# Layer one's bias added by VectorE while the product leaves PSUM, and layer two's low half split over two slots

## The chip, the cores and the metric

The kernel runs on one core of a Trainium2 chip. The metric is the device time of one execution in microseconds; lower is better. TensorE multiplies, VectorE, ScalarE and GpSimd work on tiles, SyncE issues most of the loads, and 16 DMA engines carry them.

## What is computed

Two residual blocks follow each other on x, 2048 tokens of width 512. The first is a quantised graph layer with a dense 2048 x 2048 matrix `adj`. The second, which the change touches, is a mixture of 16 experts with two chosen per token:

```python
def _L0_ffn_ref(x, Wr, br, W1, b1, g1, be1, W2, b2):
    logits = x_flat @ Wr + br
    probs = jax.nn.softmax(logits, axis=-1)
    topk_w, topk_idx = jax.lax.top_k(probs, TOP_K)
    ...
    h = jnp.einsum('nc,ech->neh', x_flat, W1) + b1
    h = _layernorm(h, g1, be1)
    h = jax.nn.gelu(h, approximate=False)
    expert_out = jnp.einsum('neh,eho->neo', h, W2) + b2
    sel = jnp.take_along_axis(expert_out, topk_idx[:, :, None], axis=1)
    ...
x = x + _L0_gnn_ref(_layernorm(x, axis=-1), adj, ...)
x = x + _L0_ffn_ref(_layernorm(x, axis=-1)[None], ...)[0]
```

All of it is float32. b1 and b2 have 16 rows of 512, one per expert.

## The kernel before

The first block takes until about 230 us and isn't touched, apart from some bias preparation beside it. Towards its end the kernel chooses experts, sorts the tokens by expert into pages of 128 and writes a plan.

The expert stage works through the pages. A page is a **slot**; this input has 40. A word of the plan, one for two slots, says which expert each slot has and whether an expert starts there. The loops run over pairs of slots: the two halves of a loop body are the slots with `par` 0 and 1, and the plan's word is read into registers at the loop's turn. `If` on a bit of that word guards the work that is done once per expert.

Precision comes from split products: a float32 factor is cut into a high part (fp32r, copied by ScalarE) and a low part (the difference, made by VectorE). A layer on a page is then 12 matmuls of 128 x 128 by 512: high by high (line 1464), low activations by high weights (line 1467), high activations by low weights (line 1470). Ahead of them, line 1462 starts the sum in PSUM with the bias: `two_rows`, which is one in two rows, times `bias_row`, a ring of four experts whose two rows hold the bias's high and low part.

**TensorE**, slot s (`slot`): transposes of `h_hat` of page s (line 1486), layer two of page s-1, transposes of the gathered rows of page s+3 (line 1455), layer one of page s+2. That order is written by hand; each group waits on semaphores.

**VectorE** has this order in slot s, by hand as well: `h_hat` of page s+1 (line 1230), low part of the gelu output of page s (1235), low part of the rows of page s+3 (1208), statistics of layer one's product of page s+2 (`slot_stats`: 1212, 1214, 1215), then `split_next`, the low half of weights (1223), for the next expert. Layer one's is made if an expert starts at slot s+2, layer two's if one starts at slot s; each is two pieces of 128 x 1024. Seen from TensorE, the statistics and pieces of VectorE's slot s come beside TensorE's slot s+1, since they wait for the product of page s+2.

**GpSimd** takes the power of the variance (line 646), gathers rows (625) and adds the outputs to memory (650). **ScalarE** has the gelu (865), the high parts (870, 824), the gated output (830) and the high halves of the weights (837), the last when the raw weights have landed and with the same conditions on starting experts.

**SyncE** loads the weights of expert e into `w_raw`, two buffers per layer, in the fixed order layer two of e, layer one of e+1, layer two of e+1, layer one of e+2. Each load waits (line 524) until VectorE has made the low half of expert e-2 of that layer (`split_lo`), and stands in the queue behind the one before it. The bias row goes ahead of each (line 472).

```python
def load_bias(n, e, ring):
    sp.dma_start(bias_row[n][0:2, ring].bitcast(F32), bias_dram[n, e]).then_inc(raw_in[n], 16)
...
def slot(s, par, word):
    slot_h_hat(s + 1, 1 - par)
    slot_g_lo(s, par)
    slot_x_lo(s + 3, 1 - par)
    slot_stats(s + 2, par)
    split_next(0, expert_in(word, par + 2), starts_in(word, par + 2))
    split_next(1, expert_in(word, par), starts_in(word, par))
```

Of the kernel before, what the change touches and what calls it, by code (L numbers as in the profile page):

```python
# [22 lines left out]
ALU = mybir.AluOpType  # L23
# [6 lines left out]
P = 128  # L30
# [137 lines left out]
def gnn_moe_program(nc, x, adj_steps, gnn_w, scalars, wr, br, w1, b1, g1, be1, w2, b2, consts, xn_rows, bias_dram, out):  # L168
    with ExitStack() as ctx:
# [87 lines left out]
        end_gnn = where[0]  # L257
        bias_row = [place(f"bias_row{n}", [P, 4 * D], F32R) for n in (1, 2)]

# [176 lines left out]
        def _(sp):  # L436
# [34 lines left out]
            def load_bias(n, e, ring):  # L471
                sp.dma_start(bias_row[n][0:2, ring].bitcast(F32), bias_dram[n, e]).then_inc(raw_in[n], 16)

# [10 lines left out]
            def store_biases():  # L484

                sp.wait_ge(bias_ok, 1)
                for n in range(2):
                    for h, half in enumerate((bias_hi, bias_lo)):
                        sp.dma_start(bias_dram[n, :, h, :], half[32 * n:32 * n + E, :].bitcast(F32)).then_inc(bias_out, 16)

# [9 lines left out]
            for n in range(2, STEPS + WINDOWS):  # L500
                sp.wait_ge(adj_lo_ok, n - 1)
                load_adj(n)
                w = n - STEPS
                if w == BIAS_OUT_IN:
                    store_biases()
                if w == WEIGHTS_IN:
                    sp.wait_ge(bias_out, 64)
                    sp.wait_ge(bias_zero, 2)
# [23 lines left out]
        def _(pool):  # L532
# [7 lines left out]
            own.link(pool.memset(b_raw[:, :], 0.0))  # L540
            for base, b in ((0, b1), (32, b2)):
                pool.dma_start(b_raw[base:base + E, :], b).then_inc(bias_in, 16)
            pool.wait_ge(consts_in, 16)
# [20 lines left out]
            for t in range(1, T):  # L564
                x_scale(t)
                if t in (AHEAD - 1, AHEAD + 1):
                    pool.memset(bias_row[(t - AHEAD + 1) // 2][:, :].bitcast(F32), 0.0).then_inc(bias_zero, 1)
            pool.wait_ge(tables_in, 16)
# [326 lines left out]
        def _(dve):  # L895
# [119 lines left out]
            def split_bias():  # L1015

                dve.wait_ge(bias_in, 32)
# [191 lines left out]

            def slot_stats(s, par):  # L1210
                dve.wait_ge(mm1, s + 1)
                link(dve.bn_stats(h_stats[:, par, :], h_ps(par)))  # L1212
                dve.sem_inc(dve_turn, 1)
# [3 lines left out]
            def split_next(n, e, start):  # L1217

                with dve.If(start == 1):
# [5 lines left out]
                    ins.then_inc(split_lo[n], 1)  # L1225

            def slot_h_hat(s, par):

                dve.wait_ge(h_rstd, s + 1)
                dve.tensor_scalar(h_hat[:, par, :], h_ps(par), h_mv[:, par, 0:1], h_rs[:, par, 0:1], ALU.subtract, ALU.mult  # L1230
                                  ).then_inc(h_hat_ok, 1)
# [5 lines left out]

            def slot(s, par, word):

                slot_h_hat(s + 1, 1 - par)  # L1240
                slot_g_lo(s, par)
                slot_x_lo(s + 3, 1 - par)
                slot_stats(s + 2, par)
                split_next(0, expert_in(word, par + 2), starts_in(word, par + 2))
                split_next(1, expert_in(word, par), starts_in(word, par))

# [4 lines left out]
            rest = dve.value_load(pairs[0:1, 0:1], min_val=E // 2 - 2, max_val=SLOTS // 2 - 2)  # L1251
            slot_stats(0, 0)
            split(1, 0, 1)
            slot_h_hat(0, 0)
            slot_x_lo(2, 0)
            slot_stats(1, 1)
            split_next(0, expert_in(word, 1), starts_in(word, 1))
            slot(0, 0, word)
            slot(1, 1, word)
            with dve.Fori(1, SLOTS // 2 - 1) as j:  # L1260
                with dve.If(j < rest + 1):
                    own.enter(j - 1, 2 * 2)
                    word = load_plan(dve, j)
                    for par in range(2):
                        slot(j * 2 + par, par, word)
                    own.leave(0)
            word = load_plan(dve, rest + 1)
            slot_h_hat(rest * 2 + 3, 1)
            slot_g_lo(rest * 2 + 2, 0)
            split_next(1, expert_in(word, 0), starts_in(word, 0))  # L1270
            slot_g_lo(rest * 2 + 3, 1)
# [4 lines left out]
        def _(pe):  # L1276
# [181 lines left out]
            def layer(dst, n, s, par, e, act_hi, act_lo, lo_ok, done):  # L1458

                at = [bass.ds((e & 1) * (C * D) + c * D, D) for c in range(C)]  # L1460
                pe.wait_ge(split_hi[n], e + 1)
                pe.matmul(dst, two_rows[:, :], bias_row[n][:, bass.ds((e & 3) * D, D)], start=True, stop=False)  # L1462
                for c in range(C):
                    pe.matmul(dst, act_hi[:, par, c * P:(c + 1) * P], w_hi[:, n, at[c]], start=False, stop=False)  # L1464
                pe.wait_ge(lo_ok, s + 1)
# [109 lines left out]
```

## Time and profile before

| | us |
|---|---|
| median of 3 runs | 531.89 |
| lowest and highest | 531.49, 533.54 |
| the profiled execution | 533.34 |
| its span, first to last instruction | 531.6 |
| mean granted TensorE clock in it | 0.967 of full |

The page gives for each engine its busy time, digits of the busy share in 40 slices of the span (13.3 us each), and groups of instructions by source line with their mean duration and the idle time ahead of them. A matmul's duration holds its way through the array, so neighbours overlap; how long it takes from the engine is the distance to the next start. Some 40 slots of the expert stage lie between 242.6 and 520 us.

### The profile page before, as it was taken

To read this page: it belongs to the slowest core of one execution; us is meant where nothing else is said; L and a number is where in the kernel's file an instruction comes from. 1 tells how busy PE (TensorE), PEld (TensorE's weight loads), DVE (VectorE), ACT (ScalarE), POOL (GpSimd) and SP (SyncE) were. 2 spreads that over 40 slices of the span, in tenths; PEclk is the share of its full clock that TensorE was granted. 3 is DMA by queue.
4 is the path that set the end of the run, shared out by engine and by line. 5 is a ranking of instruction groups with operands and counts; after the bars stand their busy time and mean duration, and the time that the engine had idled before them with its cause. 6 is when DMAs were issued, how large, how long until landed. Compare 5 with 4: busy or idle time off the path is not lost. (4 is left out here: it accounts for less than half of the span.)

```text
span 531.6 us, 10326 instructions
## 1 busy us (share of the span) xinstructions
PE 481.1 (90%) x2328; PEld 391.1 (74%) x2329; DVE 349.1 (66%) x699; ACT 289.8 (55%) x484; POOL 227.2 (43%) x302
## 2 busy tenths in 40 slices
PE   1789999899999997678999999999999999999981
PEld 0568888788877776657788788888777888778851
DVE  5797765656557568858665786676877766776420
ACT  1656453454343343526667667668768766665540
POOL 5583520411351726334544444444444444344432
PEclk9989999999999999559999999999999999999996
DMA  8621232654787441156766776776887896644443
GB/s 285 243 81 40 80 99 78 239 208 166 251 275 259 152 170 49 37 160 203 236 160 153 201 199 151 218 167 149 239 279 206 249 279 161 141 79 80 80 62 40
DMA packets 33033, 87.75 MB, mean 165 GB/s; under 512 B 6032, under 2 KB 6176, under 8 KB 32880
## 3 DMA queue, kind: packets, MB, share of 16 engines
q1 hardware_dynamic: 18912, 56.53, 32.4%
q0 software_dynamic: 9488, 22.55, 21.0%
q10 hardware_dynamic: 4608, 8.39, 4.1%
q8 instruction: 10, 0.16, 0.1%
q14 instruction: 15, 0.12, 0.1%
HBM read 68.05 MB, written 19.40 MB: 165 GB/s over the span
## 5 line engine op out<-in xcount | busy, mean ns | idle before, releaser
L865 ACT ACTIVATE g_sb<-ps,be_sb,g_sb 128x128 f32<-128x128 f32 x160 | 60.1, 456 | 63.6 <-PE ps L1486 62.9
L625 POOL DMA_INDIRECT xg<-xn_rows,tok_i x41 | 44.6, 1087 | 116.4 <-ACT gate L844 100.0
L1329 PE MATMUL ps<-sup,adj_hi 128*128 128x512 f32 x192 | 78.3, 408 | 2.3 <-DVE adj_lo L962 2.3
L1223 DVE TENSOR_TENSOR w_lo<-w_raw,w_hi x58 | 67.8, 1221 | 17.0 <-issue 17.0
L1329 PE MATMUL ps<-sup,adj_lo 128*128 128x512 f32 x192 | 75.3, 392 | 0.0
L962 DVE SCALAR_TENSOR_TENSOR adj_lo<-adj_raw,small,adj_hi 128x1024 fp32r<-128x1024 f32 x32 | 40.7, 1273 | 39.6 <-ACT adj_hi L705 39.5
L650 POOL DMA_INDIRECT out<-y_sb,scat_i x37 | 58.9, 1592 | 16.6 <-issue 10.4
L837 ACT ACTIVATE w_hi<-w_raw x29 | 54.8, 1914 | 1.8 <-DMA w_raw<-in_w 1.0
L581 POOL TENSOR_SCALAR rstd<-mv 128x1 f32<-128x1 f32 x15 | 14.6, 974 | 91.1 <-DVE mv L1008 91.1
L1230 DVE TENSOR_SCALAR h_hat<-ps,h_mv,h_rs 128x512 f32<-128x512 f32 x40 | 32.3, 807 | 28.6 <-issue 17.5
L705 ACT ACTIVATE adj_hi<-adj_raw,small 128x1024 fp32r<-128x1024 f32 x32 | 36.8, 1149 | 22.3 <-PE ps L1329 13.5
L1212 DVE BATCH_NORM_STATS2 h_stats<-ps 128x6 f32<-128x512 f32 x40 | 27.8, 696 | 28.9 <-PE ps L1470 22.2
L1329 PEld LDWEIGHTS ps<-sup,adj_hi 128*128 128x128 f32 x192 | 36.1, 188 | 11.5 <-DVE adj_lo L962 4.9
L1464 PE MATMUL ps<-w_hi,xt_hi 128*128 (+1 forms) x160 | 44.5, 400 | 0.0
L1467 PE MATMUL ps<-w_hi,xt_lo 128*128 (+1 forms) x160 | 44.3, 399 | 0.0
L1464 PE MATMUL ps<-w_hi,gt_hi 128*128 x160 | 43.5, 393 | 0.0
L1470 PE MATMUL ps<-w_lo,xt_hi 128*128 (+1 forms) x160 | 43.2, 392 | 0.0
L830 ACT ACTIVATE y_sb<-ps,gate 128x512 f32<-128x512 f32 x40 | 27.5, 688 | 28.6 <-PE ps L1470 28.6
L1470 PE MATMUL ps<-w_lo,gt_hi 128*128 x160 | 42.9, 390 | 0.0
L1467 PE MATMUL ps<-w_hi,gt_lo 128*128 x160 | 42.8, 389 | 0.0
L1329 PEld LDWEIGHTS ps<-sup,adj_lo 128*128 128x128 f32 x192 | 36.2, 188 | 6.7
L1462 PE MATMUL ps<-bias_row,two_rows 128*128 (+1 forms) x80 | 38.7, 483 | 0.1
(181 smaller groups left out, 970.4 us busy)
## 6 DMA issues: line engine op xcount, KB each, us to landing
w_raw<-in_w SPq DMA_DIRECT2D x64, 512.0 KB
adj_raw<-in_adj_steps SPq DMA_DIRECT2D x32, 512.0 KB, 3.5
out<-x_sb ACTq DMA_DIRECT2D x16, 256.0 KB, 2.9
xn_rows<-xn ACTq DMA_DIRECT2D x16, 256.0 KB, 2.8
x_sb<-in_x SPq DMA_DIRECT2D x3, 1024.0 KB, 13.5
gw_raw<-in_gnn_w SPq DMA_DIRECT2D x1, 1024.0 KB, 5.0
x_sb<-in_x SPq DMA_DIRECT2D x2, 512.0 KB, 7.6
xg<-xn_rows,tok_i POOLq DMA_INDIRECT x41, 5.5
```

The costliest lines, as they stand in the source:

```text
L625: return pool.indirect_dma_start(to[:, s % 2, :], None, xn_rows, bass.IndirectOffsetOnAxis(ap=tok_i[:, s:s + 1], axis=0)).then_inc(landed[ ...
L650: pool.indirect_dma_start(out, bass.IndirectOffsetOnAxis(ap=at, axis=0), y_sb[:, par, :], None, compute_op=ALU.add).then_inc(scattered[par ...
L705: act.activation(adj_hi[:, par, :], adj_raw[:, par, :], ACT.Copy, scale=small[:, 0:1]).then_inc(adj_hi_ok, 1)
L837: act.activation(w_hi[:, n, at], w_raw[:, n, :, :].rearrange("p a n -> p (a n)")[:, at], ACT.Copy).then_inc(split_hi[n], 1)
L865: ins = act.activation(g_sb[:, par, c * P:(c + 1) * P], ht_ps(par)[:, c * P:(c + 1) * P], ACT.Gelu, scale=g1_sb[:, bass.ds(e_s * C + c, 1) ...
L962: dve.scalar_tensor_tensor(adj_lo[:, par, :], adj_raw[:, par, :], small[:, 0:1], adj_hi[:, par, :].bitcast(F32), ALU.mult, ALU.subtract).t ...
L1223: ins = dve.tensor_tensor(w_lo[:, n, at], w_raw[:, n, :, :].rearrange("p a n -> p (a n)")[:, at], w_hi[:, n, at].bitcast(F32), ALU.subtract)
L1329: ins = pe.matmul(acc_bank(t), part[:, n % 2, k * P:(k + 1) * P], sup[:, first_k + k, :], start=first_k + k == 0 and part is adj_hi, stop= ...
L1462: pe.matmul(dst, two_rows[:, :], bias_row[n][:, bass.ds((e & 3) * D, D)], start=True, stop=False)
L1464: pe.matmul(dst, act_hi[:, par, c * P:(c + 1) * P], w_hi[:, n, at[c]], start=False, stop=False)
L1467: pe.matmul(dst, act_lo[:, par, c * P:(c + 1) * P], w_hi[:, n, at[c]], start=False, stop=False)
L1470: ins = pe.matmul(dst, act_hi[:, par, c * P:(c + 1) * P], w_lo[:, n, at[c]], start=False, stop=c == C - 1)
```

## The change

Layer one's bias no longer passes through TensorE. `b1`'s row of an expert is loaded in fp32 to all 128 partitions (`b1_rows`, a ring of four), and VectorE adds it as it takes the product out of PSUM into a new tile `h_sb`; the statistics and `h_hat` read `h_sb`. Layer two keeps its bias matmul. The preparation of high and low bias rows is left for b2 alone.

Layer two's low half, two pieces in one slot before, becomes one piece in that slot (`begin_split`, if an expert starts at slot s) and one in the next (`end_split`, if one started at slot s-1), which also signals `split_lo`. VectorE needs two words of the plan for it.

```diff
             def load_bias(n, e, ring):
-                sp.dma_start(bias_row[n][0:2, ring].bitcast(F32), bias_dram[n, e]).then_inc(raw_in[n], 16)
+                if n:
+                    sp.dma_start(bias_row[0:2, ring].bitcast(F32), bias_dram[e]).then_inc(raw_in[n], 16)
+                else:
+                    row = e if not isinstance(e, int) else slice(e, e + 1)
+                    sp.dma_start(b1_rows[:, ring], b1[row, :].broadcast_to([P, D])).then_inc(raw_in[n], 16)
...
-            for base, b in ((0, b1), (32, b2)):
-                pool.dma_start(b_raw[base:base + E, :], b).then_inc(bias_in, 16)
+            pool.dma_start(b_raw[0:E, :], b2).then_inc(bias_in, 16)
...
-                if t in (AHEAD - 1, AHEAD + 1):
-                    pool.memset(bias_row[(t - AHEAD + 1) // 2][:, :].bitcast(F32), 0.0).then_inc(bias_zero, 1)
+                if t == AHEAD + 1:
+                    pool.memset(bias_row[:, :].bitcast(F32), 0.0).then_inc(bias_zero, 1)
...
-            def slot_stats(s, par):
+            def slot_stats(s, par, e):
                 dve.wait_ge(mm1, s + 1)
-                link(dve.bn_stats(h_stats[:, par, :], h_ps(par)))
+                link(dve.tensor_tensor(h_sb[:, par, :], h_ps(par), b1_rows[:, bass.ds((e & 3) * D, D)], ALU.add))
+                link(dve.bn_stats(h_stats[:, par, :], h_sb[:, par, :]))
...
+            def low_piece(n, e, h):
+
+                at = bass.ds(((e + 1) & 1) * (C * D) + h * (C * D // 2), C * D // 2)
+                return dve.tensor_tensor(w_lo[:, n, at], w_raw[:, n, :, :].rearrange("p a n -> p (a n)")[:, at],
+                                         w_hi[:, n, at].bitcast(F32), ALU.subtract)
+
+            def begin_split(e, start):
+
+                with dve.If(start == 1):
+                    dve.wait_ge(split_hi[1], e + 2)
+                    low_piece(1, e, 0)
+
+            def end_split(e, start):
+
+                with dve.If(start == 1):
+                    low_piece(1, e, 1).then_inc(split_lo[1], 1)
...
-                dve.tensor_scalar(h_hat[:, par, :], h_ps(par), h_mv[:, par, 0:1], h_rs[:, par, 0:1], ALU.subtract, ALU.mult
+                dve.tensor_scalar(h_hat[:, par, :], h_sb[:, par, :], h_mv[:, par, 0:1], h_rs[:, par, 0:1], ALU.subtract, ALU.mult
...
-            def slot(s, par, word):
+            def slot(s, par, word, earlier):
...
-                slot_stats(s + 2, par)
+                slot_stats(s + 2, par, expert_in(word, par + 2))
                 split_next(0, expert_in(word, par + 2), starts_in(word, par + 2))
-                split_next(1, expert_in(word, par), starts_in(word, par))
+                if earlier is not None:
+                    end_split(expert_in(earlier, 1 - par), starts_in(earlier, 1 - par))
+                begin_split(expert_in(word, par), starts_in(word, par))
...
-                    word = load_plan(dve, j)
+                    earlier, word = load_plan(dve, j - 1), load_plan(dve, j)
...
-                pe.matmul(dst, two_rows[:, :], bias_row[n][:, bass.ds((e & 3) * D, D)], start=True, stop=False)
+                if n:
+                    pe.matmul(dst, two_rows[:, :], bias_row[:, bass.ds((e & 3) * D, D)], start=True, stop=False)
                 for c in range(C):
-                    pe.matmul(dst, act_hi[:, par, c * P:(c + 1) * P], w_hi[:, n, at[c]], start=False, stop=False)
+                    pe.matmul(dst, act_hi[:, par, c * P:(c + 1) * P], w_hi[:, n, at[c]], start=not n and c == 0, stop=False)
```

Three places in the instruction order. VectorE, first half of the loop body before, from the subtraction that makes `xt_lo` to the first piece of layer one's low half:

```order
L1208 TENSOR_TENSOR xt_lo<-ps,xt_hi 128x512 [waits x_hi_ok]
L1211 REGISTER_ALU
L1212 BN_STATS h_stats<-ps 128x6 [waits mm1]
L158 ISA
L1214 BN_AGGR h_mv<-h_stats 128x2 [waits dve_own]
L158 REGISTER_ALU
L1215 TENSOR_SCALAR h_rs<-h_mv 128x1 [waits dve_own]
L1219 REGISTER_ALU x2
L1219 COMPARE_AND_BRANCH
```

The same place in the changed kernel:

```order
L1212 TENSOR_TENSOR xt_lo<-ps,xt_hi 128x512 [waits x_hi_ok]
L1215 REGISTER_ALU
L1216 REGISTER_ALU [waits mm1]
L1216 REGISTER_ALU x2
L1216 ISA
L1216 TENSOR_TENSOR h_sb<-ps,b_rows 128x512
L158 ISA
L1217 BN_STATS h_stats<-h_sb 128x6 [waits dve_own]
L158 REGISTER_ALU
L1219 BN_AGGR h_mv<-h_stats 128x2 [waits dve_own]
L158 REGISTER_ALU
L1220 TENSOR_SCALAR h_rs<-h_mv 128x1 [waits dve_own]
```

An addition and its address now stand between the wait for the product (`mm1`) and the statistics, and the wait sits on a register operation.

Second, VectorE behind layer one's pieces in the same half of the loop body. `split2_hi` is the signal of ScalarE's high half of layer two. In the changed kernel:

```order
L1224 UNCONDITIONAL_BRANCH
L1246 REGISTER_ALU x2
L1246 COMPARE_AND_BRANCH
L1235 REGISTER_ALU x4
L1235 ISA
L1235 TENSOR_TENSOR w_lo<-w_raw,w_hi 128x1024
L1246 UNCONDITIONAL_BRANCH
L1240 REGISTER_ALU x2
L1240 COMPARE_AND_BRANCH
L1241 REGISTER_ALU x2
L1235 REGISTER_ALU [waits split2_hi]
```

Where one branch led to two pieces of layer two, there are two branches with a piece each, the earlier expert's second piece first, and both behind layer one's pieces.

Third, TensorE at the head of layer one in a loop body, before:

```order
L1461 REGISTER_ALU [waits x_hi_ok]
L1461 REGISTER_ALU x2
L1462 REGISTER_ALU [waits split1_hi]
L1462 ISA
L1462 MATMUL ps<-bias_row_111,two_rows 128x512
L1464 REGISTER_ALU
L1464 ISA
L1464 MATMUL ps<-w_hi,xt_hi 128x512
```

and in the changed kernel:

```order
L1486 REGISTER_ALU [waits x_hi_ok]
L1486 REGISTER_ALU x2
L1490 REGISTER_ALU [waits split1_hi]
L1490 ISA
L1490 MATMUL ps<-w_hi,xt_hi 128x512
```

The bias matmul and two register operations are gone; nothing else of the sequence moves.

## Rows read from the trace of the kernel before

**Rows 1.** The page: busy us and share; digits of the granted clock, 40 slices.

```profile
PE 481.1 (90%) x2328; PEld 391.1 (74%) x2329; DVE 349.1 (66%) x699; ACT 289.8 (55%) x484; POOL 227.2 (43%) x302
...
PEclk9989999999999999559999999999999999999996
```

**Rows 2.** A group by line from 232 us: count, busy us, mean ns.

```profile
L1208 DVE TENSOR_TENSOR xt_lo<-ps,xt_hi 128x512 fp32r<-128x512 f32 x41 | 28.1, 684 | 10.0 <-ACT xt_hi L824 9.9
```

**Rows 3.** Timeline of TensorE, three slots: start us, length us, line, count.

```profile
380.04 0.60 PE L1486 MATMUL ps<-k_sb,h_hat 128*128 128x128 f32 x4
...
380.71 1.09 PE L1464 MATMUL ps<-w_hi,gt_hi 128*128 x4
...
386.90 0.60 PE L1486 MATMUL ps<-k_sb,h_hat 128*128 128x128 f32 x4
...
389.40 1.07 PE L1470 MATMUL ps<-w_lo,gt_hi 128*128 x4
...
394.35 0.66 PE L1486 MATMUL ps<-k_sb,h_hat 128*128 128x128 f32 x4 [0.44 <-DVE h_hat L1230]
...
401.53 0.60 PE L1486 MATMUL ps<-k_sb,h_hat 128*128 128x128 f32 x4
```

**Rows 4.** VectorE, the same slots; in brackets the idle time before.

```profile
367.62 4.63 DVE L1223 TENSOR_TENSOR w_lo<-w_raw,w_hi  x4 [0.63 <-issue]
...
382.61 2.36 DVE L1223 TENSOR_TENSOR w_lo<-w_raw,w_hi  x2 [1.15 <-issue]
...
387.10 0.70 DVE L1212 BATCH_NORM_STATS2 h_stats<-ps 128x6 f32<-128x512 f32 x1 [0.21 <-issue]
...
388.17 0.15 DVE L1215 TENSOR_SCALAR h_rs<-h_mv 128x1 f32<-128x1 f32 x1
388.94 4.63 DVE L1223 TENSOR_TENSOR w_lo<-w_raw,w_hi  x4 [0.62 <-issue]
393.49 0.81 DVE L1230 TENSOR_SCALAR h_hat<-ps,h_mv,h_rs 128x512 f32<-128x512 f32 x1
...
398.63 0.81 DVE L1230 TENSOR_SCALAR h_hat<-ps,h_mv,h_rs 128x512 f32<-128x512 f32 x1 [2.01 <-POOL h_rs L646]
```

**Rows 5.** Timeline of TensorE at both ends of the 36 slots.

```profile
254.54 0.66 PE L1486 MATMUL ps<-k_sb,h_hat 128*128 128x128 f32 x4 [0.97 <-DVE h_hat L1230]
...
508.03 0.65 PE L1486 MATMUL ps<-k_sb,h_hat 128*128 128x128 f32 x4 [1.07 <-issue]
```

**Rows 6.** Line 1113: durations ns, lowest, median and highest; SBUF to SBUF.

```profile
L1113 DVE TENSOR_SCALAR xn<-x_sb,mv,rstd x1: 660/660/660, 210.9 to 210.9; 128x512 f32<-128x512 f32 x1
```

**Rows 7.** Line 419 on VectorE's sequencer, loads of the plan: ns.

```profile
L419 DVEq TENSOR_LOAD <-plan x20: 300/316/846, 233.9 to 511.9; - x20
```

**Rows 8.** Timeline of VectorE, two slots with layer two's pieces.

```profile
418.50 2.36 DVE L1223 TENSOR_TENSOR w_lo<-w_raw,w_hi  x2 [0.93 <-issue]
...
425.56 2.36 DVE L1223 TENSOR_TENSOR w_lo<-w_raw,w_hi  x2 [1.13 <-issue]
```

**Rows 9.** Timeline of SyncE's queue: weight loads.

```profile
372.87 0.81 SPq L468 DMA_DIRECT2D w_raw<-in_w  x2
...
374.73 1.91 SPq L468 DMA_DIRECT2D w_raw<-in_w  x2
```

**Rows 10.** Windows: busy us of each engine, granted clock, DMA share, GB/s.

```profile
379.80:384.80 5.00, 5.00 (x27) 4.16 (x26) 3.63 (x6) 3.56 (x8) 2.15 (x2) 1.00 0.98 293
```

**Rows 11.** Timeline of ScalarE: high halves of the weights.

```profile
385.00 3.72 ACT L837 ACTIVATE w_hi<-w_raw  x2
...
407.63 1.92 ACT L837 ACTIVATE w_hi<-w_raw  x1 [1.05 <-DMA w_raw<-in_w]
```

**Rows 12.** Windows ahead of the stage, then a row of TensorE's timeline.

```profile
209.00:212.80 3.80, 0.91 (x7) 0.57 (x6) 3.51 (x15) 1.45 (x2) 2.80 (x6) 1.00 0.10 39
212.80:220.00 7.20, 6.18 (x26) 5.70 (x26) 6.01 (x29) 3.88 (x5) 3.82 (x10) 0.50 0.17 55
...
233.38 1.91 PE L1464 MATMUL ps<-w_hi,xt_hi 128*128 128x512 f32 x4
```

More of the change, by code:

```diff
@@ L257, in gnn_moe_program @@
         end_gnn = where[0]
-        bias_row = [place(f"bias_row{n}", [P, 4 * D], F32R) for n in (1, 2)]
+        b1_rows = place("b1_rows", [P, 4 * D], F32)
+        bias_row = place("bias_row", [P, 4 * D], F32R)
+        h_sb = place("h_sb", [P, 2, D], F32)
         where[0] = end_fixed
@@ L486, in store_biases @@
                 sp.wait_ge(bias_ok, 1)
-                for n in range(2):
-                    for h, half in enumerate((bias_hi, bias_lo)):
-                        sp.dma_start(bias_dram[n, :, h, :], half[32 * n:32 * n + E, :].bitcast(F32)).then_inc(bias_out, 16)
+                for h, half in enumerate((bias_hi, bias_lo)):
+                    sp.dma_start(bias_dram[:, h, :], half[0:E, :].bitcast(F32)).then_inc(bias_out, 16)
             def first_weights(i):
@@ L506, in _ @@
                 if w == WEIGHTS_IN:
-                    sp.wait_ge(bias_out, 64)
-                    sp.wait_ge(bias_zero, 2)
+                    sp.wait_ge(bias_out, 32)
+                    sp.wait_ge(bias_zero, 1)
                 if WEIGHTS_IN <= w < WEIGHTS_IN + 8:
@@ L1015, in split_bias @@
             def split_bias():
-                dve.wait_ge(bias_in, 32)
+                dve.wait_ge(bias_in, 16)
                 link(dve.tensor_copy(bias_hi[:, :], b_raw[:, :]))
@@ L1251, in _ @@
             rest = dve.value_load(pairs[0:1, 0:1], min_val=E // 2 - 2, max_val=SLOTS // 2 - 2)
-            slot_stats(0, 0)
+            slot_stats(0, 0, 0)
             split(1, 0, 1)
@@ L1255, in _ @@
             slot_x_lo(2, 0)
-            slot_stats(1, 1)
+            slot_stats(1, 1, expert_in(word, 1))
             split_next(0, expert_in(word, 1), starts_in(word, 1))
-            slot(0, 0, word)
-            slot(1, 1, word)
+            slot(0, 0, word, None)
+            slot(1, 1, word, word)
             with dve.Fori(1, SLOTS // 2 - 1) as j:
                 with dve.If(j < rest + 1):
-                    own.enter(j - 1, 2 * 2)
-                    word = load_plan(dve, j)
+                    own.enter(j - 1, 2 * 3)
+                    earlier, word = load_plan(dve, j - 1), load_plan(dve, j)
                     for par in range(2):
-                        slot(j * 2 + par, par, word)
+                        slot(j * 2 + par, par, word, word if par else earlier)
                     own.leave(0)
-            word = load_plan(dve, rest + 1)
+            earlier, word = load_plan(dve, rest), load_plan(dve, rest + 1)
             slot_h_hat(rest * 2 + 3, 1)
             slot_g_lo(rest * 2 + 2, 0)
+            end_split(expert_in(earlier, 1), starts_in(earlier, 1))
             split_next(1, expert_in(word, 0), starts_in(word, 0))
@@ L1569 @@
     xn_rows = nc.dram_tensor("xn_rows", [N, ROW], F32, kind="Internal").ap()
-    bias_dram = nc.dram_tensor("bias_dram", [2, E, 2, D], F32, kind="Internal").ap()
+    bias_dram = nc.dram_tensor("bias_dram", [E, 2, D], F32, kind="Internal").ap()
     out = nc.dram_tensor("out", [_OUT_ROWS, D], F32, kind="ExternalOutput").ap()
```

## The prediction

> **What bounds the kernel now.** Read the page first. In [rows 1] TensorE is busy for 90% of the span and VectorE for 66%; the clock digits show 8 or 9 everywhere but in two slices near 213 to 237 us and in the last. So the expert stage, which the change touches, goes by TensorE, and a matmul taken out there is worth its place in the queue. Durations of matmuls overlap; what one takes is the distance between starts. Then read two engines beside each other, one slot (one page of 128 tokens) at a time. A slot begins with the four transposes of h_hat. On TensorE [rows 3] the slot at 380.04 ends at 386.90: 6.86 us without a gap. (Counted from 0 it is slot 20.) The last transpose, 0.11 us before its end, would hand over at about 380.47; the next product starts at 380.71: the bias takes 0.235 us. The slot at 386.90 ends at 394.35, 7.45 us, with a wait for h_hat; the one behind it takes 7.18.
>
> On VectorE [rows 4] a slot is: statistics 0.20 after the slot's start (387.10), the variance 1.07 later (388.17, ended at 1.42), the low halves of the weights where a new expert is due (first at 2.04), then h_hat for the next slot. In a slot with both layers' low halves there are four pieces, 1.135 us apart; h_hat starts at 6.59 (393.49), lasts 0.81, and TensorE, ready at 6.86, goes on at 7.45. With one layer's two pieces (382.61) there is over 1 us to spare. From 254.54 to 508.03 [rows 5] there are 36 slots; 6 have four pieces. 36 x 6.86 = 247.0 of the 253.5 us; the other 6.5 are those six and their followers, 5.3, and 1.2 at the loop's end.
>
> **The bias leaves TensorE.** 40 matmuls x 0.235 = 9.4 us, a full slot becoming 6.63. That is the whole gain, and only where TensorE still sets the slot.
>
> **The bias enters VectorE.** What is added stands between the product and the variance, so nothing behind it starts earlier. The wait now holds a register operation; three of those and one more stand before the addition. In [rows 4] nine sequencer operations lie between 388.17 and the piece at 388.94, 0.08 us each, so 0.36 here with the hand-over, where VectorE had been waiting (nothing where it is late). The addition, PSUM and SBUF to SBUF, is like the subtraction of line 1208, 0.68 [rows 2], plus the 0.15 to a linked follower: 0.83. Sum 1.19 us, bounded by 0.75 (addresses hidden) and 1.3. The statistics now read SBUF; I take no change. h_hat reads SBUF: [rows 6] has this form once, 660 ns, against 0.81 us from PSUM (393.49): 0.15 back. The Trainium skill (VectorE: DVE Perf Modes, on the mode with two read ports) says that fp32 tensor_scalar with one source runs at double rate when all lies in SBUF; by that the arithmetic would halve and some 0.27 us come back, 0.1 more per slot, an estimate from that page. The trace agrees only in direction, with 660 ns.
>
> **The third branch and the second load of the plan.** The first piece comes 0.62 us after the variance where the first branch is taken (388.94), 1.15 and 0.93 where it isn't (382.61, 418.50 [rows 4, 8]): 0.3 to 0.5 for a branch not taken. At the end of every second slot the loop turns: in the slot at 394.35, which has no pieces, h_hat started 2.16 us after the variance [rows 4]. The change reads two plan words instead of one; the load alone is 0.32 [rows 7]; I take 0.6 with its register work (bounds 0.3 and 2.16, the whole turn). In those slots h_hat can't start before about 1.27 + 1.19 + 2.16 + 0.3 + 0.6 = 5.5 without a piece, and about 6.1 with one, since its own registers come first. End 6.2 to 6.8 against 6.63: cover nearly or just gone, 0 to 0.5 us of wait in 15 slots.
>
> **VectorE slots after the change.** The pieces begin at 3.23, not 2.04. Three pieces (two of layer one and either half of layer two) give h_hat at 6.64 and a slot of 7.36; 7.85 where VectorE came late out of the slot before. The new split puts three pieces in 10 of the 36 slots (it also spreads the old fours: only the slot at 386.90 keeps four, for two halves of different experts meet there): mean 7.6, 1.0 over 6.63. The four: 9.0, so 2.4 over. The other 25: 6.63 to 7.15, on average 0.24 over, from the loop's turn and from the up to 0.32 us that a slot behind a wait takes longer (7.18 against 6.86). Sum 36 x 6.63 + 10.0 + 2.4 + 6.0 + 1.2 = 258.3 against 253.5: **+5**. At both ends of the stage, where h_hat is waited for anyway, 1.04 at the start and 1.04 + 0.6 at the end, less two matmuls: **+2**.
>
> **The second half comes a slot later, and TensorE needs it.** Beside TensorE's slots, layer two's low half for an expert is made one slot after its predecessor starts, and read in the last third of layer two, one slot after its own start. If the predecessor has one page only, nothing lies between. Two pairs are like that: layer two's pieces stand in adjacent slots at 382.61 and 388.94, and at 418.50 and 425.56 [rows 4, 8]. The expert that starts at slot 20 has its second half moved to the slot at 386.90, behind layer one's two pieces: done 3.23 + 3 x 1.135 = 6.6 after the start. TensorE wants it at 2.5 (389.40 [rows 3]) and waits 4.1, then has 4.1 us of the slot left: 10.8 in place of 9.0. The second place is the slot at 423.00: done at 4.9, wanted at 2.5, 8.8 in place of 7.1. Together **+3.5**.
>
> **The weights come later too.** SyncE refills w_raw only when that same low half is done, and layer one's next load stands behind layer two's in its queue. Loads were issued at 372.87 and 374.73 [rows 9], the first once the four pieces that start at 367.62 [rows 4] were done. The DMA engines were 98% busy up to 384.8 [rows 10], and ScalarE took layer one's half at 385.00, 5.0 after its slot's start [rows 11]: no margin. At 407.63 [rows 11] it already waited 1.05 us for DMA. After the change the releasing piece is the last of three in the following slot, 7 us later and at that slot's end, so the pair is issued at about the start of slot 20 (380.04 in the old time) and lands 12 us later, 12.9 with the row: b1's row is written to 128 partitions, 256 KB in place of 4, 0.9 us at 293 GB/s [rows 10]. ScalarE's copy of 1.92 ends at 14.8; slot 20, with one piece behind a late VectorE, lasts 7.4, so that is 7.4 into the next one; VectorE's pieces queue there behind that wait and would have begun at 3.2. h_hat and that late half are behind them: **4.1 more** in the slot at 386.90. The two loads after it shift likewise: 0.7 and 1.7 in the slots at 401.53 and 408.97. Together **+6.5**; between 0 (if the pair lands in half that time) and 10.
>
> **The clock.** In [rows 12] TensorE did 0.91 us of work in 3.8 and was then granted 0.50, its lower level of 1.2 GHz, for the next rows; four products that last 1.09 us at the full clock lasted 1.91 there. The gap above is some 8 us and a second one over 3. I take one drop with some 4 us of half-rate work, which costs 2: **+2**, range 0 to 5. The Trainium skill (TensorE: Matmul & The Clock Gate, on the gate) has the same rule, that idleness drops the array to half rate; by it alone the term would not be nothing.
>
> **Sum.** 5 + 2 + 3.5 + 6.5 + 2 = 19. The profiled execution took 533.34 (span 531.6), 1.45 above the median 531.89; I set the sum on both: 552 for an execution like the profiled one, 550 to 551 for the median. Forecast **550**. GpSimd's saved memset and the smaller bias store lie in the first stage, beside a full TensorE: nothing.
>
> **Rivals.** (1) *Loads in time.* The pair lands in well under 12 us, or the releasing piece is not later than I think: terms 6.5 and 2 go, 539 (533.5 to 541 with a cheaper chain). Against: 385.00 had no margin. (2) *The gain passes through*: the other side. If VectorE's addresses and branches run under its own arithmetic and the extra is only 0.75, h_hat stays below 6.63 outside three-piece slots; 9.4 us come off, 4 return in those slots and 1 to 3.5 at the late halves: about 527. Its point is h_hat ending before 6.6 in two-piece slots; there I find 6.2, but the late half at 386.90 follows from the order of the code. (3) *The change doesn't shed its load*: three-piece slots are as long as the old fours and both effects cancel, 530 to 534. (4) *Starvation feeds itself*: each late slot makes the next release late and the clock falls repeatedly, 560 to 570.
>
> **Chances.** Forecast 0.62 (541 to 559); loads in time 0.15; starvation 0.10; cancelled 0.08; gain 0.05. The range 536 to 562 leaves out the last two cases and most of the fourth rival's. A measurement of this kernel can tell 0.5%, 2.7 us: faster 0.05, same 0.08, slower 0.87.
>
> **What would show it.** In the new profile: a group of 40 additions near 0.69 us, h_hat near 0.66; slots of 6.6 to 6.9 with one piece or none and near 7.4 with three; a TensorE wait for w_lo of several us about 140 us into the stage and a second of some 2 us five slots on; ScalarE waiting for DMA ahead of w_hi by 5 us or more; a half-rate stretch there. Wrong if TensorE has no wait for w_lo, or if h_hat in the three-piece slots starts before 5.8.

## The result, and the profile after

| | before | after |
|---|---|---|
| median, us (4 runs each) | 531.69 | 552.63 |
| lowest and highest | 531.21, 533.54 | 550.89, 554.31 |
| the profiled execution, and its span | 533.34, 531.6 | 554.31, 552.6 |
| mean granted TensorE clock in it | 0.967 | 0.949 |

The changed kernel takes 1.0372 times as long, interval [1.0346, 1.0399]: 20 us more (21 between the two medians), where 18 were forecast. The page after, against [rows 1]:

```profile
PE 482.4 (87%) x2288; PEld 388.4 (70%) x2289; DVE 365.3 (66%) x739; ACT 289.6 (52%) x484; POOL 233.5 (42%) x300
...
PEclk9999999999999997589999989999789889999986
...
L841 ACT ACTIVATE w_hi<-w_raw x29 | 54.7, 1912 | 16.3 <-DMA w_raw<-in_w 15.8
L1496 PE MATMUL ps<-w_lo,gt_hi 128*128 x160 | 44.7, 402 | 10.8 <-DVE w_lo L1235 10.8
...
L1235 DVE TENSOR_TENSOR w_lo<-w_raw,w_hi x30 | 36.5, 1222 | 15.8 <-issue 15.8
...
L1252 DVE TENSOR_SCALAR h_hat<-h_sb,h_mv,h_rs 128x512 f32<-128x512 f32 x40 | 22.8, 569 | 30.6 <-issue 21.2
L1228 DVE TENSOR_TENSOR w_lo<-w_raw,w_hi x28 | 33.1, 1222 | 14.4 <-ACT w_hi L841 8.6
```

TensorE lost its 40 bias matmuls and has 21 us more span: its share falls from 90% to 87%. The clock digits have new dips behind the 20th slice. In the groups, the idle time ahead of an operation stands behind the second bar: 15.8 us of DMA ahead of `w_hi`, 8.6 of ScalarE ahead of layer one's low half, 10.8 of VectorE ahead of the matmuls that read layer two's low half. `h_hat` takes 569 ns.

The group of the addition, in the groups by line:

```profile
L1216 DVE TENSOR_TENSOR h_sb<-ps,b_rows 128x512 f32<-128x512 f32 x40 | 27.4, 684 | 21.3 <-PE ps L1496 20.9 <-issue 0.3
```

The addition lasts 684 ns, what line 1208 did [rows 2]. Next, where the time went. Starts of the `h_hat` transposes cut the stage into slots, counted from 0; the slot lengths, summed. The last column deals the forecast's terms out to the slots that they name (six of its ten three-piece slots lie in slots 2 to 20):

| stretch | before | after | change | forecast |
|---|---|---|---|---|
| up to slot 2 | 254.5 | 252.6 | -1.9 | with the end |
| slots 2 to 20 | 132.4 | 136.5 | +4.1 | +2.7 |
| slot 21 | 7.45 | 17.44 | +10.0 | +9.5 |
| slots 22 to 26 | 35.5 | 43.1 | +7.6 | +4.4 |
| slots 27 to 37 | 78.2 | 75.9 | -2.3 | +0.1 |
| slot 38 to the end | 23.6 | 27.0 | +3.5 | +2, both ends |

Nearly half of the loss is one slot. TensorE's timeline there, with the idle time before a row and who ended it in brackets:

```profile
389.13 0.66 PE L1512 MATMUL ps<-k_sb,h_hat 128*128 128x128 f32 x4
...
390.89 1.08 PE L1493 MATMUL ps<-w_hi,gt_lo 128*128 x4
400.81 2.04 PE L1496 MATMUL ps<-w_lo,gt_hi 128*128 x4 [8.84 <-DVE w_lo L1235]
...
406.57 0.60 PE L1512 MATMUL ps<-k_sb,h_hat 128*128 128x128 f32 x4
```

It is the slot of [rows 3] that began at 386.90. TensorE has reached the low half at 392.0, stands for 8.84 us, and takes 5.76 for what is left. Why, on the three engines before it (SyncE's queue, ScalarE, VectorE; one view each, of the same stretch):

```profile
382.29 0.82 SPq L470 DMA_DIRECT2D w_raw<-in_w  x2
...
384.23 1.82 SPq L470 DMA_DIRECT2D w_raw<-in_w  x2
```

```profile
394.94 3.71 ACT L841 ACTIVATE w_hi<-w_raw  x2 [7.43 <-DMA w_raw<-in_w]
```

```profile
397.18 2.36 DVE L1228 TENSOR_TENSOR w_lo<-w_raw,w_hi  x2 [5.07 <-ACT w_hi L841]
399.46 2.35 DVE L1235 TENSOR_TENSOR w_lo<-w_raw,w_hi  x2
401.73 0.54 DVE L1252 TENSOR_SCALAR h_hat<-h_sb,h_mv,h_rs 128x512 f32<-128x512 f32 x1
```

The loads were issued at 382.29 and 384.23, at the start of slot 20 (382.19), as forecast; ScalarE had its weights 12.65 us after the first issue and had waited 7.43 for them. VectorE's two pieces of layer one waited for ScalarE (5.07), and behind them in its queue stood the late half of layer two (the first of the two of line 1235, ended at 400.7), which needed none of these loads, and `h_hat`. The windows, with the granted clock after the busy times:

```profile
389.10:393.90 4.80, 2.87 (x14) 2.05 (x13) 2.80 (x6) 0.00 (x0) 1.70 (x2) 1.00 0.87 320
393.90:404.20 10.30, 3.39 (x10) 2.83 (x11) 5.69 (x6) 6.87 (x9) 0.49 (x1) 0.50 0.33 58
318.90:322.30 3.40, 3.40 (x10) 2.63 (x9) 2.24 (x6) 1.74 (x5) 1.62 (x2) 0.50 1.05 278
```

The granted clock was at half (1.2 GHz) for the whole second window. TensorE was idle for its first 6.9 us; the 3.4 us of work behind them lost 1.7. In the third window, 3.4 us long, TensorE was busy throughout, at half clock, and lost 1.7 too.

That third window follows a wait that the prediction didn't have. Slots 10 and 11 take 9.36 and 8.39 (6.86 each before). ScalarE, GpSimd, VectorE and TensorE in turn:

```profile
313.19 0.69 ACT L834 ACTIVATE y_sb<-ps,gate 128x512 f32<-128x512 f32 x1 [2.00 <-DMA out<-y_sb,scat_i]
```

```profile
313.92 2.33 POOL L654 DMA_INDIRECT out<-y_sb,scat_i  x1 [6.01 <-ACT y_sb L834]
315.73 1.13 POOL L650 TENSOR_TENSOR h_rs<-h_rs,k_sb 128x1 f32<-128x1 f32 x1
```

```profile
316.89 0.60 DVE L1252 TENSOR_SCALAR h_hat<-h_sb,h_mv,h_rs 128x512 f32<-128x512 f32 x1 [2.11 <-POOL h_rs L650]
```

```profile
308.19 0.60 PE L1512 MATMUL ps<-k_sb,h_hat 128*128 128x128 f32 x4
...
317.55 0.66 PE L1512 MATMUL ps<-k_sb,h_hat 128*128 128x128 f32 x4 [2.58 <-DVE h_hat L1252]
```

ScalarE can't write `y_sb` because the scatter of an earlier page still reads it. GpSimd, whose order is fixed, waits 6.01 us for that `y_sb` before it issues the next scatter, and the power of the variance (`h_rs`, 1.13) is queued behind it; so `h_hat` and TensorE wait.

### The profile page after: what moved, and what is told of

Same layout as the page of the kernel before. It is cut to its first block and busy times, and to the rows that moved or that the text cites. A ratio compares the mean times of both kernels' runs of the same rounds, so it can differ in the third digit from the quotient of the medians.

```text
span 552.6 us, 10572 instructions
## 1 busy us (share of the span) xinstructions
PE 482.4 (87%) x2288; PEld 388.4 (70%) x2289; DVE 365.3 (66%) x739; ACT 289.6 (52%) x484; POOL 233.5 (42%) x300
## 3 DMA queue, kind: packets, MB, share of 16 engines
q10 hardware_dynamic: 4608, 8.39, 4.0%
## 5 line engine op out<-in xcount | busy, mean ns | idle before, releaser
L629 POOL DMA_INDIRECT xg<-xn_rows,tok_i x41 | 48.9, 1192 | 90.5 <-ACT gate L848 61.8
L654 POOL DMA_INDIRECT out<-y_sb,scat_i x37 | 61.9, 1674 | 31.6 <-ACT y_sb L834 11.2
L841 ACT ACTIVATE w_hi<-w_raw x29 | 54.7, 1912 | 16.3 <-DMA w_raw<-in_w 15.8
L1496 PE MATMUL ps<-w_lo,gt_hi 128*128 x160 | 44.7, 402 | 10.8 <-DVE w_lo L1235 10.8
L1490 PE MATMUL ps<-w_hi,xt_hi 128*128 (+1 forms) x160 | 50.1, 437 | 0.0
L1235 DVE TENSOR_TENSOR w_lo<-w_raw,w_hi x30 | 36.5, 1222 | 15.8 <-issue 15.8
L650 POOL TENSOR_TENSOR h_rs<-h_rs,k_sb 128x1 f32<-128x1 f32 x40 | 27.8, 696 | 42.4 <-DVE h_rs L1220 42.4
L1490 PE MATMUL ps<-w_hi,gt_hi 128*128 x160 | 45.4, 407 | 0.0
L1493 PE MATMUL ps<-w_hi,gt_lo 128*128 x160 | 45.2, 407 | 0.0
L1496 PEld LDWEIGHTS ps<-w_lo,gt_hi 128*128 128x128 f32 x160 | 31.2, 196 | 18.4 <-issue 11.6
L1252 DVE TENSOR_SCALAR h_hat<-h_sb,h_mv,h_rs 128x512 f32<-128x512 f32 x40 | 22.8, 569 | 30.6 <-issue 21.2
L1228 DVE TENSOR_TENSOR w_lo<-w_raw,w_hi x28 | 33.1, 1222 | 14.4 <-ACT w_hi L841 8.6
```

What stands on the lines that cost most here:

```text
L629: return pool.indirect_dma_start(to[:, s % 2, :], None, xn_rows, bass.IndirectOffsetOnAxis(ap=tok_i[:, s:s + 1], axis=0)).then_inc(landed[ ...
L654: pool.indirect_dma_start(out, bass.IndirectOffsetOnAxis(ap=at, axis=0), y_sb[:, par, :], None, compute_op=ALU.add).then_inc(scattered[par ...
L841: act.activation(w_hi[:, n, at], w_raw[:, n, :, :].rearrange("p a n -> p (a n)")[:, at], ACT.Copy).then_inc(split_hi[n], 1)
L1228: ins = dve.tensor_tensor(w_lo[:, n, at], w_raw[:, n, :, :].rearrange("p a n -> p (a n)")[:, at], w_hi[:, n, at].bitcast(F32), ALU.subtract)
L1235: return dve.tensor_tensor(w_lo[:, n, at], w_raw[:, n, :, :].rearrange("p a n -> p (a n)")[:, at], w_hi[:, n, at].bitcast(F32), ALU.subtract)
L1493: pe.matmul(dst, act_lo[:, par, c * P:(c + 1) * P], w_hi[:, n, at[c]], start=False, stop=False)
```

## The experiments

Times are medians; ratios are against the kernel before on the same chip, with the 95% interval. A slot is long or short by the same count as above.

**Each half of the change alone.** First the ceiling: `before` without the bias matmul of layer one, and without b1.

```diff
-                pe.matmul(dst, two_rows[:, :], bias_row[n][:, bass.ds((e & 3) * D, D)], start=True, stop=False)
+                if n:
+                    pe.matmul(dst, two_rows[:, :], bias_row[n][:, bass.ds((e & 3) * D, D)], start=True, stop=False)
```

> The kernel before with layer one's bias matmul left out and nothing in its place: b1 isn't added at all, so the output differs. Theory (a matmul's place is 0.235 us, and TensorE sets every slot but the six with four pieces): 34 x 0.235 = 8.0 us less, 523 to 524. Rival A (the place is the 0.32 us from the bias matmul's start to the next one's): 11 less, 521. Rival B (VectorE already sets the pace in most slots): under 3 less, 529 or more.

525.14, ratio 0.9885 [0.9829, 0.9942]. Slots are 6.63 in place of 6.86, but the six with four pieces stay at 7.45. TensorE at the end of one of them:

```profile
388.43 0.66 PE L1487 MATMUL ps<-k_sb,h_hat 128*128 128x128 f32 x4 [0.67 <-DVE h_hat L1230]
```

Taking out 9.4 us of TensorE's work is worth 8.0 by the medians and 6.1 by the ratio, whose interval allows 3 to 9; the 36 slots of the profiled execution give 6.8. VectorE keeps the rest. (That slot is 7.46 long, the wait 0.67.)

The bias alone: `after`, with both pieces of layer two back in one slot.

```diff
-                if earlier is not None:
-                    end_split(expert_in(earlier, 1 - par), starts_in(earlier, 1 - par))
-                begin_split(expert_in(word, par), starts_in(word, par))
+                split_next(1, expert_in(word, par), starts_in(word, par))
```

> The changed kernel with layer two's low half put back into one slot: the bias part of the change alone. Theory (the addition lengthens VectorE's chain by some 1.1 us ahead of h_hat, which is more than the 0.235 it gives TensorE in slots with pieces): slots with four pieces 8.4 us or so in place of 7.45, two-piece slots near 6.7, no TensorE wait for w_lo; 2 to 5 us slower than before, 534 to 537. Rival (the addition runs under cover, and TensorE's 9.4 us pass through): 524 to 528.

535.17, ratio 1.0037 [1.0019, 1.0055]. VectorE in a four-piece slot:

```profile
364.44 0.69 DVE L1216 TENSOR_TENSOR h_sb<-ps,b_rows 128x512 f32<-128x512 f32 x1 [1.48 <-PE ps L1493]
...
367.00 4.63 DVE L1228 TENSOR_TENSOR w_lo<-w_raw,w_hi  x4 [0.61 <-issue]
371.55 0.54 DVE L1252 TENSOR_SCALAR h_hat<-h_sb,h_mv,h_rs 128x512 f32<-128x512 f32 x1
```

From the addition to the first piece 2.56 us, in [rows 4] 1.84 from the statistics (387.10 to 388.94); the six four-piece slots go from 7.45 to between 8.09 and 8.61, 5.1 us together. The light slots, most of them 0.23 shorter, give some 6 and both ends take 3; slot 27 is 1.5 longer, of which below. In the waits of this kernel TensorE has none for `w_lo`.

The split alone: `before`, with `low_piece`, `begin_split`, `end_split` and the two plan words of the diff.

> The kernel before with layer two's low half in two pieces in two successive slots, the bias still a matmul: the other part alone. Theory (late second half behind two experts of one page, and weight loads released a slot later): TensorE waits for w_lo at two places, some 3 us or more at the first, ScalarE waits for the weights' DMA over 3 us at the first; 5 to 10 us slower, 537 to 542. With the bias part this leaves 7 us or more of the 21 as interplay (the late half stands behind a longer VectorE chain). Rival (spreading the four pieces is worth its 5 us and the bias part is what costs): at or below 531.

540.58, ratio 1.0133 [1.0098, 1.0168]. The waits between 254 and 532 (total, number, longest) and TensorE's timeline:

```profile
ACT w_hi L837 <- DMA w_raw<-in_w: 10.3, 3, 5.2
...
PE ps L1490 <- DVE w_lo L1230: 7.4, 2, 6.6
```

```profile
392.03 2.05 PE L1490 MATMUL ps<-w_lo,gt_hi 128*128 x4 [6.61 <-DVE w_lo L1230]
```

The split does what it says: four of the six four-piece slots fall from 7.45 to 6.87 (slot 23 to 7.18, and slot 21 keeps its four). It also brings both the wait for the late half and the late loads by itself: slot 21 is 16.55, with 6.61 of waiting and some 3.2 lost to half clock, which was granted from 387.9 to 398.3, over 6.3 us of TensorE's work. The halves cost 2.0 and 7.1 us; together 20. So about 11 us come only when both are there: slots 10 and 11 are 7.00 and 7.07 with the split alone, 6.65 and 6.63 with the bias alone, and 9.36 and 8.39 with both; slot 26 is 7.94, 6.63 and 10.40.

**Are the loads to blame?** `after`, with the weight loads from expert 2 on cut to 8 of 128 partitions; every wait stays. The control makes the same cut in `before`.

```diff
-            def load_half(n, h, at, par):
-                sp.dma_start(w_raw[:, n, par,
...
+            def load_half(n, h, at, par, rows=P):
+                sp.dma_start(w_raw[0:rows, n, par,
...
-                    load_half(n, h, at, par)
+                    load_half(n, h, at, par, 8)
```

> The changed kernel with every weight load from expert 2 on cut to 8 of 128 partitions (the rest of the weights is stale, so the output differs); waits, signals, order and b1's row of 256 KB are as they were. Theory of the forecast (late weight loads cost 6.5 us and the clock behind them 2): ScalarE no longer waits for DMA ahead of w_hi, the slot of 17.4 us falls to 11 or 12, where TensorE waits some 4 us for the late half alone; about 544. Addition to it (the load bursts, now later, also hold up the scatters, which is what makes the slots of 9.4 and 8.4 us that the forecast doesn't have): these slots return to 7.5 or less as well, 537 to 540. Rival (the wait of the long slot is the order of VectorE's pieces alone): 550 or more.

> The kernel before with the same cut of the weight loads to 8 partitions (stale weights, the output differs): what the cut is worth where loads are released in time. Theory: at most 1 us, 530.5 to 532; the four-piece slots stay at 7.45. Rival (the DMA bursts cost something everywhere): 528 or less.

540.24, ratio 1.0145 [1.0095, 1.0195], and the control 532.19, 0.9994 [0.997, 1.0017]: size of loads is nothing to `before` and 12.4 us to `after`. The waits of the first between 380 and 402, then TensorE at slots 10 and 11:

```profile
PE ps L1497 <- DVE w_lo L1236: 4.3, 1, 4.3
...
ACT w_hi L842 <- DMA w_raw<-in_w: 0.9, 1, 0.9
```

```profile
308.35 0.60 PE L1513 MATMUL ps<-k_sb,h_hat 128*128 128x128 f32 x4
...
315.49 0.66 PE L1513 MATMUL ps<-k_sb,h_hat 128*128 128x128 f32 x4 [0.33 <-DVE h_hat L1253]
```

The time is at the edge of what was expected with the scatters included (537 to 540), 4 us below what was expected by the late loads alone (544). ScalarE's wait falls from 7.43 to 0.93, and the late half costs 4.29 by itself: 4.1 had been forecast. Slot 21 is 12.64, slot 10 7.14 and slot 11 6.78: the held scatters of slot 10 were the loads' doing.

**Is it the place behind layer one's pieces?** `after`, with the late half ahead of them.

```diff
                 slot_stats(s + 2, par, expert_in(word, par + 2))
-                split_next(0, expert_in(word, par + 2), starts_in(word, par + 2))
                 if earlier is not None:
                     end_split(expert_in(earlier, 1 - par), starts_in(earlier, 1 - par))
+                split_next(0, expert_in(word, par + 2), starts_in(word, par + 2))
```

> The changed kernel with layer two's second piece ahead of layer one's pieces in its slot, not behind them. It is then done 2.27 us earlier in the slots that have all three, and doesn't stand behind the wait for layer one's high half; the loads that it releases go 2.27 us earlier. Theory: TensorE's wait for w_lo in the long slot falls from 8.8 to 1 to 2 us, the slot lasts 10 to 12 us, VectorE still waits there for w_hi; 542 to 546. Rival (the release of the loads alone decides): wait unchanged within 2.3 us, 549 or so.

543.95, ratio 1.0214 [1.0116, 1.0312]. TensorE's wait for the late half is 2.04, slot 21 10.72:

```profile
395.45 1.44 PE L1496 MATMUL ps<-w_lo,gt_hi 128*128 x4 [2.04 <-DVE w_lo L1235]
```

The place behind layer one's pieces is worth 6.7 us in slot 21. How much in all is open: 8.7 by the medians, but this kernel ran only twice, with 547.27 and 540.63, so 5 to 12. The edit should also release the loads 2.27 us earlier, and no run parts the two. Slot 10 is still 9.20.

**A version that moves layer two's pieces as a pair.** `before`, with layer two's pair made behind `xt_lo` and ahead of the statistics. The expert's word is that of the slot before, so the pair is ready 1.9 us later than in `before` (8.58 in place of 6.67 after the start of slot 18), but lies where VectorE used to wait for TensorE, and not in the chain from statistics to `h_hat` of that slot.

```diff
                 slot_x_lo(s + 3, 1 - par)
+                if earlier is not None:
+                    split_next(1, expert_in(earlier, 1 - par), starts_in(earlier, 1 - par))
                 slot_stats(s + 2, par)
                 split_next(0, expert_in(word, par + 2), starts_in(word, par + 2))
-                split_next(1, expert_in(word, par), starts_in(word, par))
```

> The kernel before, bias still a matmul, with both of layer two's pieces moved as a pair behind h_hat, gt_lo and xt_lo, ahead of the next statistics: not in the way of h_hat, yet done within the first third of the slot in which they may be needed. Theory (the six four-piece slots cost 5.3 us because the pieces stand ahead of h_hat, and a low half is late only when it is done after 2.5 us of a slot): no slot over 7.0, 4 to 5 us faster, 526 to 528. Rival (any later release of the weight loads costs, since the load at 385.00 had no margin): 531 or more, with ScalarE waiting for DMA over 3 us.

528.94, ratio 0.9933 [0.9911, 0.9955]: faster than both kernels, by a little less than expected. VectorE at an old four-piece slot:

```profile
363.80 2.36 DVE L1223 TENSOR_TENSOR w_lo<-w_raw,w_hi  x2 [0.62 <-issue]
366.08 0.81 DVE L1230 TENSOR_SCALAR h_hat<-ps,h_mv,h_rs 128x512 f32<-128x512 f32 x1
...
368.00 2.35 DVE L1223 TENSOR_TENSOR w_lo<-w_raw,w_hi  x2
```

Layer one's pair, `h_hat` on time, then layer two's pair. But for slots 22 to 24 (7.58, 8.02, 7.16) and slot 37 at the loop's end (8.14; 8.08 before), none is over 7.03. The rival's sign is there in part: ScalarE waits for DMA 3.9 us in all, 2.0 at the longest.

**The same place with the bias on VectorE:** `after` with this order.

> The changed kernel with the bias on VectorE, but layer two's low half as a pair behind xt_lo and ahead of the addition, as in the moved version of the kernel before. Theory (no piece but layer one's stands ahead of h_hat, so two-piece slots end near 5.9 and TensorE keeps its 6.63 in most slots; VectorE is then over 85% full, and where pairs follow each other the next slot starts late; weight loads are released some 2 us later than before): 36 slots in about 247 to 252 us, 524 to 531 in all. Rival (VectorE as a whole is full, and the order no longer matters): 534 or more, as with the bias part alone.

535.49, ratio 1.0055 [1.0031, 1.0078]. That missed. ScalarE and TensorE about slot 27 (9.67 us), and the waits for loads:

```profile
435.72 0.69 ACT L834 ACTIVATE y_sb<-ps,gate 128x512 f32<-128x512 f32 x1 [3.06 <-DMA out<-y_sb,scat_i]
```

```profile
439.27 1.12 PE L1511 MATMUL ps<-k_sb,h_hat 128*128 128x128 f32 x4 [2.89 <-DVE h_hat L1252]
...
440.62 1.79 PE L1489 MATMUL ps<-w_hi,gt_hi 128*128 x4
```

```profile
ACT w_hi L841 <- DMA w_raw<-in_w: 8.4, 3, 3.9
```

It is slot 10 again (and slot 27 of `e_bias_only`, where GpSimd waited 5.2 us for `y_sb`): a scatter held, `h_rs` behind GpSimd's 7.05 us wait for `y_sb`, TensorE 2.89 late and then at half clock (1.79 us for products that last 1.09). The rival has its share too: in slots 22 and 23 (9.51 and 8.60) the pair stands ahead of the addition and the loop's turn behind it, and with small loads, below, they still are 8.15 and 8.60.

Whether earlier loads of layer one help, I tried with the order in SyncE's queue turned (layer one of e+1 ahead of layer two of e):

```diff
             load_static(0, 2)
+            load_static(0, 3)
...
-in ((1, 0), (0, 1), (1, 1), (0, 2)):
+in ((1, 0), (0, 2), (1, 1), (0, 3)):
```

> The moved version of the kernel before (bias still a matmul), with SyncE's queue put in the order in which the loads are needed: layer one of expert e+1 ahead of layer two of e. Theory (the slots of 7.6 and 8.0 us that the moved version still had come from layer one's load standing behind layer two's, whose release is now 2 us later): those two slots at 7.0 or less, ScalarE waits for DMA under 1 us in all, 1 to 2 us faster than the moved version, 526 to 528. Rival (these slots come from scatters that land late): 528 to 530, the wait of ScalarE's output copy for the scatter remains.

> The same queue order in the version with the bias on VectorE and the pair moved. Theory (its slots of 9.5, 8.6, 9.7 and 8.0 us come partly from late loads, partly from a full VectorE): 3 to 5 us faster than 535.5, 530 to 533, still no faster than the moved version without the bias. Rival (loads are all that is in the way of the 8 us that the bias matmul costs): 525 or less.

> The version with the bias on VectorE and the pair moved, with weight loads from expert 2 on cut to 8 of 128 partitions (stale weights, the output differs): the bound without any late load. Theory (VectorE keeps some slots long where pairs follow each other, and the stage's end is 1 to 3 us longer): 527 to 530. Rival (late loads are all that stands in the way): 524 or less.

The first: 530.38, ratio 0.9948 [0.9929, 0.9968]. The theory fell: ScalarE no longer waits for DMA, and slots 22 and 23 are 7.99 and 8.02 (7.58 and 8.02 in the old queue order). VectorE there:

```profile
392.40 2.35 DVE L1224 TENSOR_TENSOR w_lo<-w_raw,w_hi  x2
394.67 0.69 DVE L1213 BATCH_NORM_STATS2 h_stats<-ps 128x6 f32<-128x512 f32 x1
...
398.46 0.81 DVE L1231 TENSOR_SCALAR h_hat<-ps,h_mv,h_rs 128x512 f32<-128x512 f32 x1 [2.58 <-issue]
```

The pair delays the statistics to 394.67, and then comes the loop's turn, with 2.58 us in which VectorE waits for nothing but its own instructions. The second: 531.83, ratio 0.9987 [0.9962, 1.0012], as expected; the new queue order takes 3.7 us off the version with the bias. The third has small loads and the old queue order: 529.38, ratio 0.9935 [0.9914, 0.9957]. Even with loads that are never late, the bias on VectorE is worth no more than leaving it on TensorE (528.94).

## Why the prediction was right, and where only by luck

550 was forecast and 552.63 measured, inside the range. The mechanism held; the sum came out by errors that cancel: VectorE's chain was put 6.4 us too high, the clock 4.8 too low, and 3.3 weren't in it at all. With `e_small_loads` as the kernel in which loads are never late, the stage's slots 2 to 37 (before 253.5, after 272.9, small loads 257.4) fall apart into the terms:

- **VectorE's chain: forecast +5, measured about -1.4.** 257.4, less 3.5 for the two late halves (the forecast's own 1.8 and 1.7, since slots 21 and 26 came out as long as it has them) and 1.8 for the clock in slot 21, is 252.1. This is the term that failed in size. In slot 16, with three pieces:

```profile
354.34 0.69 DVE L1216 TENSOR_TENSOR h_sb<-ps,b_rows 128x512 f32<-128x512 f32 x1 [0.61 <-PE ps L1496]
...
356.76 2.36 DVE L1228 TENSOR_TENSOR w_lo<-w_raw,w_hi  x2 [0.48 <-issue]
359.04 1.23 DVE L1235 TENSOR_TENSOR w_lo<-w_raw,w_hi  x1
360.19 0.53 DVE L1252 TENSOR_SCALAR h_hat<-h_sb,h_mv,h_rs 128x512 f32<-128x512 f32 x1
```

  The slot began at 353.67: the first piece comes 3.09 in (forecast 3.23), `h_hat` at 6.52 (6.64), and it lasts 0.53 where I took 0.66. So the addition with its addresses put off the first piece by 1.05, not by 1.19. The next slot starts after 7.11 us, not 7.36; slot 32 after 7.09. The ten slots with three pieces make 3.6 of the 6.4 us: they average 7.3, where I had 7.6. The other 2.6 are spread over the light slots. I had taken `h_hat`'s 660 ns from one instruction of another place [rows 6]; the 40 of the new kernel mean 569. The estimate from the Trainium skill (VectorE: DVE Perf Modes, on the mode with two read ports), which I had put beside it and not used, was 0.27 us back against 0.81; measured is 0.24.
- **Light slots with the loop's turn: held.** Slot 34, one piece and the turn, has `h_hat` 5.90 in (forecast 6.1), and takes 6.67.
- **The late halves: +3.5, held.** 4.29 us of waiting in slot 21 with loads out of the way (forecast 4.1); less the clock's 1.8 that slot is 10.84 (forecast 10.8), and slot 26 in that kernel is 8.84 (forecast 8.8).
- **The late loads: forecast +6.5, measured 7.2.** Without the clock: 17.44 against 12.64 in slot 21 is 4.8 (forecast 4.1), 9.36 against 6.94 in slot 24 is 2.4, where ScalarE waited 5.15 us for DMA. Issue at the slot's start and some 12.7 to landing were right. Slot 23, for which I had 0.7, is 8.33 with large loads and 8.31 with small ones.
- **The clock: forecast +2, measured 6.8.** Half clock was granted four times in these slots, 1.7 us each: in slots 11, 21, 25 and 26, each time behind a wait. It was granted twice more at the ends, of which below. I had seen that the first drop would come, and given the repetition to the fourth rival. That the clock falls repeatedly is what happened, at a smaller price than its 560; that each late slot makes the next release late isn't shown.
- **Not forecast: +3.3**, the held scatters in slots 4, 10 and 11, which with small loads are 5.0 us shorter, 1.7 of it the clock. The prediction followed the loads to `w_raw` and never asked who else is on the DMA engines. Either half of the change alone has none of it in these slots, and each has it once, in slot 27 (8.37 with the bias alone, 7.94 with the split alone; GpSimd's wait for `y_sb` 5.2 and 5.0 us). So neither the longer chain nor the later release is needed for it; why it falls on slots 4, 10 and 11 with both is open.
- **The ends: forecast +2, measured +1.6, by luck.** The time up to slot 0 is 2.3 shorter, which isn't due to the change: it lies between 240.35 and 242.81 in these kernels, whatever they change (the wait for `h_hat` ahead of slot 0, 2.11 in place of 1.36, is in it). Slots 0 and 1 add 0.4: slot 0 is 5.29 in place of 3.91, as in every kernel with the bias on VectorE, and each of them was granted half clock there (some 1.6 us of it); slot 1 is 7.00 in place of 8.01, as with the split alone (6.89). Behind slot 38 it is +3.5. TensorE waits 3.22 for `h_hat` in place of 1.48, which is the forecast's +1.6 for this end. Half clock behind that wait costs another 1.5: TensorE needs 5.17 us from there to its next page, 3.67 before. So the clock cost about 10 us in all. VectorE at that wait, before and after:

```profile
512.61 0.81 DVE L1230 TENSOR_SCALAR h_hat<-ps,h_mv,h_rs 128x512 f32<-128x512 f32 x1 [4.39 <-issue]
```

```profile
526.73 0.15 DVE L1220 TENSOR_SCALAR h_rs<-h_mv 128x1 f32<-128x1 f32 x1
532.14 0.60 DVE L1252 TENSOR_SCALAR h_hat<-h_sb,h_mv,h_rs 128x512 f32<-128x512 f32 x1 [5.25 <-issue]
```

  `h_hat` is late there by VectorE's own instructions, and most of that was there before: 4.39 us, 4.38 with the bias alone, 5.30 with the split alone. The split's second plan word and branch add 0.9.

Sum: -1.4 + 3.5 + 7.2 + 6.8 + 3.3 + 1.6 = 21.0, against 21.0 between the spans. The slots are those of one profiled execution each (small loads with a span of 538.1 us, the changed kernel with 552.6), so a term is good to some tenths of a us. What remains open: which of the instructions at the loop's exit take VectorE's 4.4 us.

The rivals: *loads in time* (539) is what `e_small_loads` shows, at 540.24, and in the real kernel ScalarE's 7.43 us rules it out. *The gain passes through* is ruled out by `e_bias_only`, which is 2 us slower than `before`, and by the wait in slot 21; but it was nearer than I thought, since the chain term alone is a small gain. *Cancelled* comes near `e_bias_only` (535.17, against its 530 to 534), not the whole.

## What to carry to other kernels

When a step that releases a buffer is moved later, follow the release, not the step: the half that moved cost 3.5 us by itself, and 12 more through the loads that waited for it, half clock and held scatters included. Before work is delayed to lighten a slot, look for idle time in which it could be done at nearly the same time: with the bias left on TensorE that version was faster (0.9933), the delayed one slower (1.0133). And work taken from the busiest engine is worth what the engine that receives it has to spare in its fullest slots, not on average: VectorE was busy for 66%, and the bias was worth nothing there.

## What the runs showed of the hardware

- A scatter's read of its source was held by other traffic. With two pairs of weight loads issued from 299.93 and 301.88 on, the DMA engines were this busy:

```profile
302.00:312.90 10.90, 10.90 (x55) 9.05 (x55) 8.39 (x15) 7.35 (x14) 2.98 (x3) 1.00 0.93 267
```

  and ScalarE got `y_sb` back at 313.19, just as the traffic ended. GpSimd stood 6.01 us for it; with small loads (`e_small_loads`) it has no such wait there.
- Work on VectorE's sequencer shows as "issue": in `before` 4.39 us at the loop's exit, and 1.8 to 2.5 at those turns of the loop where `h_hat` has no piece ahead of it. Either is more than a piece of 128 x 1024 fp32 (1.22).
- `h_hat`, fp32 128 x 512 with two scalars by pointer, takes 569 ns from SBUF and 0.81 us from PSUM [rows 4]; the addition with one operand in PSUM takes 684.
- What half clock cost did not follow the length of the wait ahead of it: 1.7 us behind 8.84 in slot 21 and behind 1.96 in slot 26 of the changed kernel, some 3.2 behind 6.61 in `e_split_only`, where it was still granted for 6.3 us of work.
